# Hand-over between two parts of a graph network: the first group's attention moved into the drain of the first part

## The reference

```python
h = relu(layernorm(x))
x = x + gat8(h, adj)                 # 8 heads, masked softmax over the neighbours, relu
h = relu(layernorm(x))
for l in range(3):                   # second part
    s = si[:, :, None] + sj[:, None, :] + attn_b[l]     # si, sj: two dot products with each row
    attn = softmax(where(mask, leaky_relu(s), -inf))
    u = layernorm(h + attn @ h) * g1[l] + beta1[l]
    ff = gelu(u @ W1[l] + b1[l]) @ W2[l] + b2[l]
    h = layernorm(u + ff) * g2[l] + beta2[l]
out = x + h
```

## Time and profile before

| what | value |
|---|---|
| median of 3 runs | 1604.88 us (1604.13 to 1605.83) |
| profiled execution | 1605.96 us |
| its span | 1604.1 us |
| TensorE busy | 1512.8 us (94%) |
| VectorE busy | 1346.0 us (84%) |
| ScalarE busy | 1091.7 us (68%) |
| GpSimd busy | 898.5 us (56%) |
| granted TensorE clock, mean | 0.982 of full |

### The profile page before, as it was taken

One profiled execution on the slowest core, in us unless ns is written; L12 is line 12 of the kernel. 1 busy time (PEld: TensorE's weight loads), 2 busy tenths in 40 slices (PEclk: granted clock), 3 DMA queues, 4 the chain that ended last, 5 costly groups with the idle time before them and its releaser, 6 DMA issues. The chain is left out here.

```text
span 1604.1 us, 37352 instructions
## 1 busy us (share of the span) xinstructions
PE 1512.8 (94%) x11360; PEld 1274.0 (79%) x11360; DVE 1346.0 (84%) x4302; ACT 1091.7 (68%) x1946; POOL 898.5 (56%) x1008
## 2 busy tenths in 40 slices
PE   5999999489999999989999999899999999999995
PEld 5667777378888888878888888788888888888884
DVE  2899999888889898968898989698988888898952
ACT  1688888457676767656777666577677666767663
POOL 1688999535453646544636465536455564546364
PEclk9999999789999999999999999999999999999998
DMA  6343343610000112110001121000011110000001
GB/s 189 84 156 119 129 130 116 193 35 8 14 15 10 45 37 71 47 28 9 14 19 36 37 70 48 28 8 14 24 31 49 58 60 14 13 9 15 8 27 53
DMA packets 70896, 83.02 MB, mean 52 GB/s; under 512 B 29264, under 2 KB 54096, under 8 KB 70736
## 3 DMA queue, kind: packets, MB, share of 16 engines
q1 hardware_dynamic: 69104, 74.76, 16.0%
q0 software_dynamic: 816, 3.15, 0.7%
q10 hardware_dynamic: 816, 3.15, 0.5%
HBM read 38.95 MB, written 25.17 MB: 40 GB/s over the span
## 5 line engine op out<-in xcount | busy, mean ns | idle before, releaser
L830 ACT ACTIVATE bank<-bank,b_col 128x512 f32<-128x512 f32 x384 | 252.9, 659 | 359.3 <-PE bank L768 358.9
L780 PE MATMUL bank<-w_hi,hid_hi 128*128 128x256 f32 x1536 | 443.5, 289 | 16.1 <-DVE hid_lo L992 12.7
L780 PE MATMUL bank<-w_hi,hid_lo 128*128 128x256 f32 x1536 | 434.7, 283 | 0.0
L780 PE MATMUL bank<-w_lo,hid_hi 128*128 128x256 f32 x1536 | 432.6, 282 | 0.0
L992 DVE TENSOR_TENSOR hid_lo<-bank,hid_hi 128x512 fp32r<-128x512 f32 x384 | 259.3, 685 | 144.1 <-ACT hid_hi L835 140.4
L780 PEld LDWEIGHTS bank<-w_hi,hid_hi 128*128 128x128 f32 x1536 | 289.7, 189 | 52.4 <-DVE hid_lo L992 39.7
L768 PE MATMUL bank<-nT_hi,w_hi 128*128 128x512 f32 x768 | 317.2, 413 | 8.2 <-issue 5.1
L768 PE MATMUL bank<-nT_lo,w_hi 128*128 128x512 f32 x768 | 305.4, 398 | 4.7 <-issue 4.7
L768 PE MATMUL bank<-nT_hi,w_lo 128*128 128x512 f32 x768 | 305.0, 397 | 0.0
L780 PEld LDWEIGHTS bank<-w_lo,hid_hi 128*128 128x128 f32 x1536 | 289.7, 189 | 10.1
L780 PEld LDWEIGHTS bank<-w_hi,hid_lo 128*128 128x128 f32 x1536 | 289.2, 188 | 0.0
(11 more groups left out here) (122 smaller groups left out, 3069.4 us busy)
## 6 DMA issues: line engine op xcount, KB each, us to landing
raw_weights<-xin SPq DMA_DIRECT2D x96, 128.0 KB, 2.4
xin<-in_x_dram SPq DMA_DIRECT2D x16, 512.0 KB, 4.0
first_block_out<-x_res SPq DMA_DIRECT2D x16, 512.0 KB, 2.7
second_block_in<-x_act SPq DMA_DIRECT2D x16, 512.0 KB, 3.7
xin<-second_block_in SPq DMA_DIRECT2D x16, 512.0 KB, 3.9
x_fin<-first_block_out SPq DMA_DIRECT2D x16, 512.0 KB, 3.9
out_dram<-x_fin SPq DMA_DIRECT2D x16, 512.0 KB, 2.9
xh_other<-xh SPq DMA_DIRECT2D x128, 33.0 KB, 1.9
```

The lines of the kernel that those rows point to most:

```text
L780: mm = pe.matmul(FF[t // 2][:, (t % 2) * D:(t % 2 + 1) * D], a[:, r, t * P:(t + 1) * P], w[:, l, c, :], start=(c == 0 and t % 2 == 0 and p ...
L830: act.activation(h[:], h[:], ACT.Gelu, bias=b1_col[:, l, c:c + 1]).then_inc(s_gelu, 1)
```

## The change

In the kernel before, the drain hooks held three steps of the second part on VectorE (the dot products of group 0 after steps 70 and 71, `diagonal(0, 0)` after step 72) and one on TensorE (`spread(0, 0)` after step 73). The change starts the dot products after step 68 and puts the following behind the drain steps:

| after step | VectorE | TensorE | ScalarE |
|---|---|---|---|
| 68 | dots of group 0, first half | | |
| 69 | dots, second half; `diagonal(0, 0)` | | |
| 70 | `scores(0, 0)` | `spread(0, 0)` | |
| 71 | dots of group 1, first half | | `exp(0, 0)` |
| 72 | row sums, residual, statistics of slot 0 | `turn_attn(0, 0)` | `keep_attn(0, 0)` |
| 73 | dots of group 1, second half; `diagonal(0, 1)` | `aggregate(0, 0)` | |

Beside this, `scores(0, 1)` on VectorE is moved behind `split_n(0, 0)`, and GpSimd's `c1_row` waits until `scores(0, 1)` is done (`s_sh` at 2). No operation is added or taken away.

```diff
--- before.py
+++ after.py
@@ -783,15 +783,17 @@
                     mm.then_inc(s_ff, 1)
 
                 def tail(tau):
-                    if tau == NT + 9:
+                    if tau == NT + 6:
                         pe.wait_ge(s_samer, 1)
                         pe.wait_ge(q_ev, NT)
                         spread(0, 0)
+                    if tau == NT + 8:
+                        turn_attn(0, 0)
+                    if tau == NT + 9:
+                        pe.wait_ge(q_vh, 2 * NT)
+                        aggregate(0, 0)
 
                 def before():
-                    turn_attn(0, 0)
-                    pe.wait_ge(q_vh, 2 * NT)
-                    aggregate(0, 0)
                     spread(1, 1)
                     turn_n(0, 0)
                     pe.wait_ge(s_whi, 4 * L + NT - HEAD)
@@ -862,9 +864,13 @@
                         act.wait_ge(s_nT, KD * V + k + 1)
                         act.copy(nT_hi[:, s % 2, k, :], NT_B[k][:]).then_inc(s_nhi, 1)
 
+                def tail(tau):
+                    if tau == NT + 7:
+                        exp(0, 0)
+                    if tau == NT + 8:
+                        keep_attn(0, 0)
+
                 def before():
-                    exp(0, 0)
-                    keep_attn(0, 0)
                     norm_n(0, 0)
                     first_part_over(act)
                     split_n(0, 0)
@@ -892,7 +898,7 @@
                 def after(U):
                     norm_y(U, (SLOTS - 1) % 2, range(TG))
 
-                first_scalar(act, lambda tau: None)
+                first_scalar(act, tail)
                 slots(act, before, some, after)
 
             def second_gpsimd(pool):
@@ -956,6 +962,7 @@
                     scale_n(0)
                     pool.wait_ge(s_rows, 16 * 3)
                     pool.wait_ge(s_b, 32)
+                    pool.wait_ge(s_sh, 2)
                     pool.tensor_tensor(c1_row[:], c1_row[:], b2_row, ALU.add).then_inc(s_c1, 1)
                     pool.wait_ge(s_c1, 1)
                     pool.wait_ge(s_g2, 32)
@@ -1119,28 +1126,31 @@
                 def tail(tau):
                     if tau == NT:
                         dve.tensor_copy(same_graph_r[:], same_graph[:]).then_inc(s_samer, 1)
-                    if tau == NT + 6:
+                    if tau == NT + 4:
                         dve.wait_ge(s_w2lo, NT - HEAD)
                         dve.wait_ge(s_rows, 16 * 3)
                         dots_of(0, 0, range(0, 2))
+                    if tau == NT + 5:
+                        dots_of(0, 0, range(2, 4))
+                        diagonal(0, 0)
+                    if tau == NT + 6:
+                        scores(0, 0)
                     if tau == NT + 7:
-                        dots_of(0, 0, range(2, 4))
+                        dots_of(0, 1, range(0, 2))
                     if tau == NT + 8:
-                        diagonal(0, 0)
+                        row_sums(0)
+                        row_invs(0)
+                        residual(0, 0)
+                        stats_n(0, 0)
+                        spread_n(0)
+                    if tau == NT + 9:
+                        dots_of(0, 1, range(2, 4))
+                        diagonal(0, 1)
 
                 def before():
-                    scores(0, 0)
-                    dots_of(0, 1, range(0, 2))
-                    row_sums(0)
-                    row_invs(0)
-                    residual(0, 0)
-                    stats_n(0, 0)
-                    spread_n(0)
-                    dots_of(0, 1, range(2, 4))
-                    diagonal(0, 1)
-                    scores(0, 1)
                     first_part_over(dve)
                     split_n(0, 0)
+                    scores(0, 1)
                     dots_of(0, 2, range(TG))
                     diagonal(0, 2)
 
```

## The result

The changed kernel takes 1606.23 us (median of 20 runs, 1605.07 to 1610.42), the kernel before 1604.32 (20 runs, 1601.88 to 1605.87). The medians differ by 1.9 us. The ratio of all runs is 1.0015, 95% interval 1.0009 to 1.0022: slower by 2.4 us, with 1.4 to 3.5 as its interval. The profiled execution took 1606.85, its span is 1605.0.

The account below looks back on a forecast made before the run. TensorE, 94% busy, was taken as the bound, with the start of output(0, 0), set by VectorE's low, deciding. 0.8 + 2.4 - 0.4 = +2.8 us gave 1608.8 profiled, 1607.7 on the median; range 1601.5 to 1610.3.

Parts of the forecast that it names:

- Most of the gain is lost on ScalarE: Drain: scores(0, 0) ends 4.2 us earlier, but keep_attn(0, 0) waits behind step 72's x_act, leaving ve_a 1.6 us earlier.
- The stalls come back on the dots: VectorE before output(0, 0): stalls of 1.58 and 1.06 us return on group 2's dots, making output(0, 0) 0.8 us later.
- One wait per GpSimd instruction: Group 2's dots on VectorE: 1.4 us beside c1_row and 0.93 for each of four others, 5.1 in sum.
- the two ends: Bounds on the stall of group 2's dots beside GpSimd: 2.05 us from below, 7.2 from above.
- the strict form of the lock: GpSimd also waits some 0.35 us for each dot; dots end about 1 us later, sum 1.0 higher; not adopted.
- the rows' pitch: Spacing of GpSimd's make_base instructions in the profile, 1.33 and 1.345 us, kept for the estimate of the dots.
- The clock: TensorE waits 5.4 us before output(0, 0), its clock falls and it restarts at half rate: 2.4 us lost, 0.4 regained.
- The 2.4: Loss in us from the lower clock behind output(0, 0), taken below the 2.8 of a full 5.6 us return.
- The 0.4 that TensorE was to regain in its later waits: Part of the clock loss got back from 0.9 us idle in the first 28.5 us after output(0, 0).
- The first return of the clock: TensorE's rise to 2.4 GHz after hidden(0, 0) begins, put at 5.6 us after it, about 329.
- Other edits at no cost: c1_row's data come at about 324.5, before the scores release it at 325.5, so nothing waits; cover 1 us.

Follow-up runs that it names:

- D: Changed kernel with turn_attn(0, 0) a step earlier, keep_attn(0, 0) right behind exp(0, 0), aggregate(0, 0) after step 72: 1605.9 us, 1.0012 of the kernel before.
- A: Changed kernel with GpSimd's five instructions (c1_row, first make_base) put behind scale_n(1) and the new wait on s_sh removed: 1601.6 us, 0.9986 of the kernel before.
- E: Kernel before with GpSimd's addition of the bias rows and make_base(0) put behind scale_n of slot 1, no other edit: 1601.5 us, ratio 0.9983.
- B: Changed kernel with scores(0, 1) put ahead of split_n(0, 0) and first_part_over again: 1606.4 us, 1.0015 of the kernel before.
- C: Changed kernel without GpSimd's new wait on s_sh for scores(0, 1): 1606.8 us, 1.0019 of the kernel before.
- G: Changed kernel with 24 small products (128x64) in TensorE's idle time ahead of spread(1, 1): 1600.1 us, 0.9976 of the kernel before; again 1599.6, 0.9972.
- H: Kernel before with 24 products of 128x64 in TensorE's idle time ahead of spread(1, 1), nothing else: 1597.3 us, ratio 0.9960.

## Why the prediction was right

The forecast was +2.8 us, slower or the same; measured is +2.4 (1.4 to 3.5), and 3.0 between the two traces counted from z. Its steps, counted from the end of step 68, against the trace:

| step | predicted | measured |
|---|---|---|
| `scores(0, 0)` over | 12.5 | 12.7 |
| `keep_attn(0, 0)` over | 16.6 | 16.6 |
| `ve_a` | 22.7 | 22.7 |
| `hidden(0, 0)` | 29.9 | 29.8 |
| dots of group 2 begin | 31.9 | 31.7 |
| their length | 8.8 | 9.2 |
| `output(0, 0)` | 43.7 | 43.9 |
| wait in front of it | 5.4 | 5.9 |
| lower clock behind it | 5.6 | 5.7 |

- *Most of the gain is lost on ScalarE* (right, D): ScalarE in the changed kernel has `keep_attn` right behind the `x_act` that stands ahead of it.

```profile
307.30 0.60 ACT L428 ACTIVATE x_act<-x_res,nmr,rstd 128x256 f32<-128x256 f32 x1 [2.57 <-POOL nmr L483]
307.80 0.35 ACT L854 COPY raw_weights<-bank 128x256 f32<-128x256 f32 x1
```

- *The stalls come back on the dots* (right, A and E): +0.8 forecast, +1.05 measured. One wait per GpSimd instruction was the right choice between the two ends. The four make_base instructions grew only from 1.34 to 1.39 us on the mean (2.68 for two and 2.87 for two). By the strict form of the lock, as in the Trainium skill's "SBUF — State Buffer", section "Who interferes with whom", the dots should have ended 1 us later than the forecast; they ended 0.3 later (z + 40.9 for z + 40.7), so the measurement decides for the rows' pitch.
- *The clock* (mechanism right, one term mis-sized): the fall and the return are in the trace as forecast. The 2.4 was 2.56. The 0.4 that TensorE was to regain in its later waits is the term that failed: under 0.1 came back in the 355 us up to the loop's first turn, and the 0.5 more by which the rest shrinks to 1.96 came off at the turns and behind them, where two traces of one kernel differ by up to 2.3. So 1.05 + 2.5 = 3.5 was the price at the first turn, and that the whole comes near 2.8 owes something to luck. Half of 5.7 would be 2.85; the products lost 2.56, since at the low clock they follow each other in 0.21 (128x256) and 0.43 us (128x512), at the full clock in 0.12 and 0.23, which is less than double. The first return of the clock was misjudged as well, without effect on the sum: it came at 324.1, 2.8 us after `hidden(0, 0)` began, not 5.6.
- *Other edits at no cost* (right, barely): `c1_row` was released by the scores, not by its rows, but `make_base` waited 0.32 us for the last of its rows.
- What I did not see: that the largest lever for a kernel with effects of this size lay in the place of TensorE's loop code, and that once `output(0, 0)` starts earlier than some z + 40, part of what is won goes into the next waits (A). Neither touched the sum, since the change moves no instruction on TensorE past the loop's start.

The rest is longer than in the kernel before in A to E as well, by 1.1 to 2.4 us in one trace each. In B, C and D it is the low clock, in A the wait at 348.92. In E only 0.4 of 1.4 arises ahead of the first turn. What each turn adds, and how much of it is chance, stays open.

## What to carry to other kernels

An earlier start of a chain is worth only what its last partner can follow: here TensorE began 4.5 us earlier and met a VectorE whose list of work ahead of the awaited instruction was no shorter. When work on GpSimd is put off so that it does not disturb one VectorE instruction, look at what stands there instead; the wait moves. It can be put beside instructions that read one input from PSUM (`nT_lo` took 0.65 us beside `make_base`) or behind the one that TensorE waits for (A, E). A wait of TensorE between dense stretches can cost more than its length: behind waits of 3.7 to 5.9 us the products ran at 1.2 GHz for a while, and the 1.5 to 2.6 us were not made up in later waits. And before a difference of a few tenths of a per cent is put down to an edit on an engine with a loop, run a control that only moves its code.

## What the runs showed that I had not expected

TensorE stands at each turn of its loop for 2.0 to 2.9 us with no releaser, and in some layouts a second time, one product later, for another 1.9 to 2.7. 24 products more ahead of the loop, in either of the two places tried, take the second stand away in all seven traces, and with it 6 to 7 us of 1604 (G against the changed kernel, H against the kernel before). Only this one shift was tried.

The profile ties the stands to the instruction queue q8, whose transfers are of 16384 bytes. Its packets, MB and share of the DMA engines from 694 to 702 us, in the kernel before and then in that of H:

```profile
q8 instruction: 2, 0.03, 1.7%
```

```profile
q8 instruction: 2, 0.03, 1.8%
```

In the kernel before they start at 695.09 and 698.46, where TensorE's stands start at 695.16 and 698.58; in H at 694.70 and 697.82, where its one stand starts at 695.32. So it is at all 28 turns of the 14 traces: one transfer starts up to 0.7 us ahead of the first stand, a second 0.3 to 1.0 us after TensorE has gone on, with a second stand or without. Both layouts have the second transfer; in one TensorE stands for it, in the other it works on. This is a tie in time: the view does not name the engine that a queue serves, and no run moved a transfer by itself. The Trainium skill, "Runtime: NRT & Kernel Launch", section "Instruction fetch mechanics", has a mechanism that fits: instructions are fetched ahead in blocks of 16 KB, and a taken branch whose target is outside of what is held stops the engine until it has come. That a target just ahead of a block's end would stop it twice is my inference from this.
